# Head attention started with two groups of heads on one chunk, and lengths, statistics and last products moved in both attention layers

## The reference, cut to what matters

```python
x = x + attn_a(layernorm(x))   # 16 heads of 16; q = k = v = the normalised x, causal, softmax
x = x + ffn(layernorm(x))      # a mixture: the 2 best of 8 experts per batch, gelu
x = x + attn_b(layernorm(x))   # exp(-distance squared) of q and k, softmax over that, times v, output weights
x = x + ffn(layernorm(x))      # the same mixture again
# attn_a: w = q k^T / 4, masked to k <= q; softmax(w) v
```

## Time and profile before

| | |
|---|---|
| median of 3 runs | 1738.57 us (1738.33 to 1741.73) |
| the profiled execution, by the same clock as the runs | 1740.63 us |
| its span in the profile | 1738.9 us |
| head attention, first to last exponential | 13.5 to 532.0 us |
| first mixture | to 899 us |
| distance attention | 899 to 1367 us |
| second mixture and stores | to 1738.9 us |
| busy: PE, DVE, ACT, POOL | 97%, 59%, 55%, 18% |

### The profile page before, as it was taken

The page is one execution under the profiler, slowest core; times in us unless marked ns, Lnnn a source line. Parts: engine busy times, 40 slices in busy tenths (PEclk is TensorE's granted clock), DMA queues, the critical chain, the costliest instruction groups (busy, mean ns, idle before and its releaser), DMA issues.

```text
span 1738.9 us, 27945 instructions
## 1 busy us (share of the span) xinstructions
PE 1691.6 (97%) x10527; PEld 1156.4 (66%) x10527; DVE 1018.2 (59%) x2136; ACT 952.2 (55%) x1262; POOL 305.6 (18%) x402
## 2 busy tenths in 40 slices
PE   5999999999999999999999999999999999999998
PEld 2222222222226888888878889889899888888887
DVE  6342333344327755865566687766887886575554
ACT  4999999999996222422235444554444432243222
POOL 2022112212210000000014335434334200000000
PEclk9999999999999999999999999999999999999999
DMA  4000000100120011000000000000000200300000
GB/s 134 19 14 19 22 17 13 25 14 13 26 98 1 1 51 48 1 1 1 0 1 1 1 1 1 1 1 1 1 1 25 73 1 1 121 13 13 13 12 25
DMA packets 33697, 35.91 MB, mean 21 GB/s; under 512 B 3271, under 2 KB 30494, under 8 KB 33566
## 3 DMA queue, kind: packets, MB, share of 16 engines
q1 hardware_dynamic: 33566, 34.14, 6.6%
HBM read 22.07 MB, written 4.19 MB: 15 GB/s over the span
## 4 chain that ended last, share of the span: by engine, by line
PE 76%; ACT 11%; issue 7%; DVE 4%; POOL 0%; DMA 0%; ACTq 0%; DVEq 0%; POOLq 0%
ACT a_probs L579 10%; PE f_h L816 7%; PE f_ypsum L818 7%; PE f_ypsum L816 7%; PE a_out L386 7%; PE f_ypsum L817 7%; PE f_h L818 7%; PE f_h L817 7%; PE a_scores L700 4%; PE d_outs L816 4%; PE d_outs L817 4%; PE d_outs L818 4%; PE d_banks L816 3%; PE d_banks L818 3%; PE d_banks L817 3%
## 5 line engine op out<-in xcount | busy, mean ns | idle before, releaser
L579 ACT ACTIVATE a_probs<-a_scores 128x1024 f32<-128x1024 f32 x544 | 500.3, 1178 | 16.8 <-PE a_scores L700 16.6
L1167 ACT ACTIVATE f_gelu<-f_h,f_bcol 128x512 f32<-128x512 f32 x256 | 176.6, 690 | 467.6 <-PE f_h L818 461.2
L386 PE MATMUL a_out<-a_probs,a_values 128*32 128x512 f32 (+3 forms) x2560 | 296.0, 544 | 6.3 <-DVE a_moving L460 2.8
L1227 DVE TENSOR_SCALAR f_hh<-f_gelu,f_gates 128x512 fp32r<-128x512 f32 x256 | 124.8, 488 | 236.7 <-ACT f_gelu L1167 235.3
L1665 ACT ACTIVATE d_score<-d_dist,d_nksq 128x512 f32<-128x512 f32 x128 | 92.8, 725 | 218.9 <-DVE d_dist L1808 217.1
L1229 DVE SCALAR_TENSOR_TENSOR f_hl<-f_gelu,f_gates,f_hh 128x512 fp32r<-128x512 f32 x256 | 192.5, 752 | 9.2
L700 PE MATMUL a_scores<-a_moving,a_fixed 64*128 64x512 f16 (+3 forms) x1280 | 184.5, 355 | 9.2 <-ACT a_probs L579 4.0
L1702 POOL TENSOR_TENSOR distance_raw<-distance_raw,d_p 128x512 f32<-128x512 f32 x112 | 146.1, 1304 | 193.7 <-ACT d_p L1640 193.6
L593 POOL TENSOR_SCALAR_AFFINE_SELECT a_probs<-a_probs 128x256 f32<-128x256 f32 (+1 forms) x224 | 98.5, 455 | 431.0 <-ACT a_probs L579 428.9
L700 PEld LDWEIGHTS a_scores<-a_moving,a_fixed 64*128 64x128 f16 x1280 | 48.8, 94 | 174.6 <-ACT a_probs L579 139.3
L816 PE MATMUL f_h<-c_xhi,f_w 128*128 128x512 f32 x384 | 155.2, 404 | 0.1
(11 more groups left out here) (235 smaller groups left out, 2970.7 us busy)
## 6 DMA issues: line engine op xcount, KB each, us to landing
f_raw<-in_L_ffn_W SPq DMA_DIRECT2D x24, 512.0 KB, 7.7
a_fixed<-a_moving SPq DMA_DIRECT2D x60, 96.0 KB, 2.3
x<-in_L_attn_a_x SPq DMA_DIRECT2D x7, 512.0 KB, 8.9
out<-x SPq DMA_DIRECT2D x7, 512.0 KB, 2.9
f_raw<-in_L_ffn_W SPq DMA_DIRECT2D x12, 256.0 KB, 3.5
a_fixed<-a_moving SPq DMA_DIRECT2D x60, 32.0 KB, 2.0
f_early_raw<-in_L_ffn_W SPq DMA_DIRECT2D x4, 256.0 KB, 3.4
x<-in_L_attn_a_x SPq DMA_DIRECT2D x2, 256.0 KB, 2.8
```

Source lines behind the costliest of these rows:

```text
L386: mm = pe.matmul(spare[32 * j:32 * j + 32, i % 2, skip:skip + w], values[:, G % 2, kt + tile, j, :], probs[:, u % UR, j % 2, col:col + w], ...
L579: act.activation(probs[:, u % UR], scores[:, 2 * (u % SR):2 * (u % SR) + 2, :], ACT.Exp, scale=HD ** -0.5)\
L1167: act.activation(gel[:, n % HR, :], hps[:, n % 2, :], ACT.Gelu, bias=mix.bcol[:, q, FT * e + j:FT * e + j + 1])\
L1227: dve.tensor_scalar(hh[:, n % HR, :], gel[:, n % HR, :], gate, None, ALU.mult).then_inc(s_hh, 1)
```

## The change

1. `outputs` now begins (0,0), (1,0): the first chunk of the second group (other heads, the same tokens) is job 1 and output 1; the rest follows as before. `number` gives the place of a (`G`, `c`).
2. The `fixed` side of job 1 is copied by DVE (`place_fixed`, new semaphore `s_pfix1`) and no longer by ACT; ACT's `high_fixed(1)` stands ahead of the first unit. A chunk's steps wait for `fixed` only at its diagonal ("first"), no longer at its first full step.
3. `spare_free` is replaced by `free(bank)`, with a list of readers for each of the two banks. `TURN_AT` and the new `FIRST_TURN_AT` turn the jobs at other steps; job 2 is turned in a scores bank.
4. SP issues `copy_fixed(2)` ahead of the loads of batch 1.
5. DVE's program is written in another order: statistics, splits and places at other gaps. The statistics, norm and gathering of batch 0 stand at outputs 18, 19, 22 and 23; before they stood at 17, 19, 21, 23 and 25. A split no longer stands between a chunk's place and its `copy_out` but behind `copy_out`.
6. Distance attention: `lengths(0)` behind turn(3); several other lengths a step later, or behind a projection; the statistics of batch 0 three steps earlier (steps 73 on; before 76 on).
7. The last two weighted products (`DRAIN` = 2) are left to `finish`: one behind `up(0)`, one behind `up(1)` of the second mixture, and the denominator behind the second.

```diff
-        outputs = [(G, c) for G in range(NG) for c in range(CHUNKS)]
+        outputs = [(0, 0), (1, 0)] + [(G, c) for G in range(NG) for c in range(CHUNKS) if (G, c) not in ((0, 0), (1, 0))]
+        number = {of: i for i, of in enumerate(outputs)}
...
-        STATS_AT = {done + 1: range(TILES // 2), done + 3: range(TILES // 2, TILES)}
-        NORM_AT = done + 5
-        GATHER_AT = {done + 7: range(TILES // 2), done + 9: range(TILES // 2, TILES)}
-        MEAN_AT, CHOOSE_AT = done + 9, done + 11
+        STATS_AT = {done + 2: range(TILES // 2), done + 3: range(TILES // 2, TILES)}
+        NORM_AT, GATHER_AT, MEAN_AT, CHOOSE_AT = done + 6, done + 7, done + 9, done + 11
...
-        FIRST_TURN_AT = {5: 2, 7: 3}
-        FIRST_OUT_AT = 9
+        TURN_AT = {15: (0, (0, 1)), 16: (0, (2, 3)), 17: (1, (0,)), 18: (1, (1,)), 19: (1, (2,)), 21: (1, (3,)),
+                   26: (2, (0,)), 27: (2, (1,)), 28: (2, (2,)), 29: (2, (3,)), 30: (3, (0,)), 31: (3, (1,)), 32: (3, (2,)), 33: (3, (3,))}
+        FIRST_TURN_AT = {11: (3, (0, 1)), 12: (3, (2, 3)), 19: (4, (0,)), 20: (4, (1,)), 21: (4, (2,)), 22: (4, (3,)),
...
             load_batch(pr, sp, 0)
+            copy_fixed(BY_ENGINES)
             load_batch(pr, sp, 1)
...
             place(0)
-            statistics(1, late)
-            first_norm.rest(dve, TPC, 2 * TPC)
             normalise(1)
             halves(1)
             low_fixed(1)
+            statistics(1, late)
+            place(1)
+            first_norm.guess(dve, TPC, 2 * TPC)
+            place_fixed()
+            for i in range(3):
+                first_norm.newton(dve, i)
+            split(2)
+            copy_out(0)
+            place(2)
             statistics(2)
-            place(1)
+            finish_out(0)
+            copy_out(1)
             first_norm.rest(dve, 2 * TPC, 3 * TPC)
-            copy_out(0)
-            split(2)
...
+            finish_out(1)
             split(3)
...
+            def free(bank):
+                for s_read, count in reads[bank]:
                     pe.wait_ge(s_read, count)
+                reads[bank].clear()
...
                 if tiles[0] == 0:
-                    spare_free()
+                    if job == 2:
+                        pe.wait_ge(s_exp, 8)
+                    else:
+                        free(bank_of(job))
+                        reads[bank_of(job)].append((s_emov, job + 1))
                     pe.wait_ge(s_lo, job + 1)
...
+                if n == 1:
+                    turn(1)
                 if n == 2:
-                    turn(1)
                     turn_fixed(1)
+                if n == 5:
+                    turn(2)
...
-    LAG = 4
+    LAG, DRAIN = 4, 2
...
-              4: [("turn", 5), ("lengths", 3), ("norm", 6)],
-              5: [("values", 3), ("project", 4, 0), ("norm", 7)],
+              4: [("turn", 5), ("norm", 6)],
+              5: [("values", 3), ("lengths", 3), ("project", 4, 0), ("norm", 7)],
...
-              88: [("lengths", 15)],
+              89: [("lengths", 15)],
...
-            lengths(0)
             turn(3)
+            lengths(0)
             values(0)
-            for n in range(STEPS + LAG):
+            for n in range(STEPS + LAG - DRAIN):
...
-                if 12 <= at < 12 + TILES // 2:
+                if 9 <= at < 9 + TILES // 2:
...
-                if at == 20:
+                if at == 17:
                     next_norm.guess(dve)
...
         def finish(pe, part):
-            if part == 0:
+            weighted(pe, STEPS - DRAIN + part)
+            if part == DRAIN - 1:
                 pe.wait_ge(mix.s_bcol, 1)
                 denominator(pe, NG - 1)
```

More of the change, by code:

```diff
@@ L408, in _ @@
             distance_inputs.load(sp)
[L409 removed]
+            for job in range(BY_ENGINES + 1, CHUNKS * NG):
                 copy_fixed(job)
@@ L534, in _ @@
                         mix.part_low(dve, 0, part)
-                if i == CHUNKS + 1:
-                    for s_chunk in pr.s_x[1]:
-                        dve.wait_ge(s_chunk, 16)
-                    second_norm.whole(dve)
-                if i in STATS_AT:
-                    dve.wait_ge(s_added, CHUNKS * GROUPS)
-                    for t in STATS_AT[i]:
-                        next_norm.stats(dve, t)
-                if i == NORM_AT:
-                    next_norm.rest(dve)
-                    routing.shift(dve)
-                for t in GATHER_AT.get(i, ()):
-                    routing.gather(dve, t)
-                if i >= 1:
-                    copy_out(i)
-                    finish_out(i)
+                copy_out(i)
+                if more and c == 1:
+                    split(behind)
+                if more and c == 2:
+                    split(behind + 2)
+                if i == 2:
+                    first_norm.rest(dve, 3 * TPC, TILES)
+                finish_out(i)
                 if i == MEAN_AT:
@@ L665, in turn_fixed @@
                 mm.then_inc(s_tfix, 1)
-                routed.append((s_pfix, job + 1))
+                if job == 0:
+                    reads[1].append((s_pfix, 1))
             def turn_out(i):
-                spare_free()
+                free(i % 2)
+                reads[i % 2].append((s_added, i + 1))
                 pe.wait_ge(s_ocopy, i + 1)
```

237 lines of the change are left out of this document (132 added, 105 removed).

## The result

| | before | changed |
|---|---|---|
| median of 4 runs each, in one session | 1739.38 us (1738.33 to 1741.73) | 1726.4 us (1726.1 to 1728.75) |
| ratio of the runs | | 0.9924, interval 0.9912 to 0.9936 |
| the profiled execution, its span | 1740.63, 1738.9 us | 1726.31, 1724.3 us |
| first exponential, unit 23, table load behind the last exponential | 13.54, 48.52, 532.04 | 13.70, 38.55, 520.22 |
| first projection, last `d_dist` of the distance attention | 899.06, 1358.41 | 887.20, 1343.50 |

Faster by 0.76%, 13.0 us by the medians. Between the two profiles each landmark moved further from the one before: 10.0 up to unit 23, 1.8 from there to the last exponential, 3.05 in the distance attention, -0.3 at its end, 14.6 in all.

What follows compares the result with a forecast made beforehand. ACT was taken to bound head attention, PE distance attention. 8.9 + 1.9 + 1.7 - 0.1 = 12.4 us gained: 1728.2 from the profiled 1740.63, 1726.2 from the median 1738.57. Range 1722.8 to 1733.2.

Steps and rivals of the forecast that it cites:

- start, to unit 23: Start of head attention: 13.9 us lost before, 5.0 still lost in the new order, so 8.9 us gained.
- holes at 409 and 431: Two later ACT holes in head attention, 0.81 + 1.05, both go: 1.9 us gained, between 0 and 2.5.
- distance attention: Waits at lengths(0), (3) and (15) shrink by 0.45, 0.6 and 1.0, less 0.35: 1.7 us gained, between -1 and 2.7.
- its end: End of distance attention: DVE's chain behind the denominator is unchanged, 0.1 us lost; bounds 1.4 gained and 1.25 lost.
- u7 waits for products(1), which is as long again: 0.9: Start: the second group's unit 7 waits for PE's products(1), costing ACT 0.9 us.
- split(2) ends at 22.5 and doesn't decide: Start: DVE's split for job 2 ends at 22.5 and does not set unit 10, forecast at 26.1.
- the 1.2 that I worked out from the Trainium skill: Start: by the DVE and GpSimd port lock, about 1.2 us more lost, making the sum 7.7.
- Both causes are moved to chunks of 20 us and more: Holes at 409 and 431: the gathering and the late split move to long chunks, 1.9 us gained.
- The 0.35 for the earlier norm: Distance attention: 0.35 us taken off because batch 0's norm moves beside a chunk's results on DVE.
- the first (PE at 1.2 GHz in the start): Rival: PE stays at 1.2 GHz to u18, 5 of the 8.9 gone, gain 7, 1731.5 us; chance 0.16.
- PE is the bound: Rival: PE, not ACT, bounds head attention; gain 2 from the distance attention only, 1736.5 us; chance 0.07.
- Slower: Rival: the rest of the table is late in each head-attention group, 3.8 us worse, 1742.4 us; chance 0.05.

Runs made afterwards that it cites:

- kernel 8: The changed kernel with the second half of the gathering of batch 0 back ahead of the copy_out of output 25: 1726.17 us.
- experiment 5: The changed kernel with each chunk's first step, full or diagonal, waiting for that chunk's fixed side again: 1741.77 us, ratio to before 1.0014.
- the kernel at the end of 11: The changed kernel with DVE's guess of the norm ahead of place(1) and the first Newton step ahead of place_fixed: 1725.73 us.
- experiment 10: The changed kernel with the last job of each group turned at steps 32 to 35 as before, not 30 to 33: 1729.1 us.
- kernels 8, 9 and 10: Kernel 8, experiment 10 and, between them, the changed kernel with one list of readers for both spare banks: 1728.1 us.
- experiment 3: The changed kernel with the statistics and norm of batch 0 in the distance attention back three steps later: 1726.51 us.
- kernel 6: The kernel before, with jobs 2 to 31 awaiting their fixed side at the chunk's diagonal, not its first step: 1740.93 us, ratio 1.0006.

## Why the prediction was right, and where its steps were not

The forecast 1726.2 against 1726.4 is closer than its terms, and that much is luck. Term by term, by the two profiles:

| term | predicted | measured |
|---|---|---|
| start, to unit 23 | 8.9 | 10.0 (8.2 in the other course) |
| holes at 409 and 431 | 1.9 | 1.8 |
| distance attention | 1.7 | 3.05 |
| its end | -0.1 | -0.3 |
| sum | 12.4 | 14.6 |

- **The start, right in its mechanism.** The second group's first units fill the time in which the second chunk is made ready. This is read from the trace, where the old holes are gone; no run here undoes the order of `outputs` alone. Unit 5 at 19.6 was 19.66, partly by luck: I took 0.8 for a turn of eight transposes, though the earlier trace rows has 1.06 for one, and 1.9 for the products; measured from start to start they are 0.97 and 0.96 for the two turns (15.32 and 16.83) and 1.44 for the products (17.79). In the nine profiles with this start unit 5 lies between 18.9 and 20.0. "u7 waits for products(1), which is as long again: 0.9" failed: PE was at its higher pace by then (products at 19.77 take 1.07). "split(2) ends at 22.5 and doesn't decide" failed: it ended at 23.1, and PE waited 1.02 for it. Unit 10 came 0.8 sooner than forecast, unit 23 0.75 (38.55 for 39.3); the last wait was for `place(3)`, as forecast. In kernel 8's course unit 23 came at 40.3, so the 39.3 lies between the two.
- **What I gave no price**: that the fixed side is awaited at the diagonals. I let unit 10 follow its place at once and didn't say that this rests on the second item of the change. It carries 15 us (experiment 5). A reader of my sum could have thought that the swap alone does it.
- **DVE and POOL.** Beside masks the norm's L178 took 0.36 and not 0.17, Newton's first instruction 0.59 and not 0.16, and the normalise of four tiles 1.17 and not 0.97. These add 0.8, two thirds of the 1.2 that I worked out from the Trainium skill ("SBUF — State Buffer", on the lock of the shared port); the trace agrees with the rule, and one Newton step, not three, met a mask. (In the kernel at the end of 11, three were slowed: 0.41, 0.32 and 0.62 for 0.16.)
- **The holes.** The size was right. "Both causes are moved to chunks of 20 us and more" was wrong for the first: the eight last tiles still stand ahead of a `copy_out` (experiment 8 moves them at no gain), and what took the hole away was the turn two steps sooner (experiment 10). What took the second hole away I didn't test. It did not come back in kernels 8, 9 and 10, so it was not the place of the gathering's second half, the separate banks or the turns of the last job; the split, now ahead of `finish_out` and the mean, remains, not shown by a run. In the trace of before, DVE waits 1.89 for the mean's sums, up to 428.02, and only then makes the split at 428.10 that PE waits for the earlier trace rows.
- **The distance.** `lengths(0)` 0.48 for 0.45 and `lengths(15)` 1.06 for 1.0 were right; `lengths(3)` gave 0.30 for 0.6, as values(3) now waits 0.89 for DVE's copy. The 0.35 for the earlier norm was wrong, it costs nothing (experiment 3). Not counted at all were 6, 7, 13 and 14, together 1.2: I looked for waits that the timeline puts in brackets, and three of these four have none; one sees them only in the distance from start to start.
- **The end** was right: DVE's chain behind the denominators decides, no gain from the move. As forecast, PE's wait now stands ahead of down(0) (0.24) and up(4) (1.03). Up(4) starts 6.89 behind the denominator and not 6.61 as before, which is the 0.3.
- **The profile and the median.** I took the profiled execution to stand 2.06 above the median. Over all sessions before's medians are 1739.4 to 1740.2, so it stood 0.4 to 1.2 above, and the changed kernel's profiled execution stands at its median. By the clock of the runs the two profiled executions lie 14.3 apart (14.6 by their spans), so my terms fell short by 1.9; this and the 2.06 taken off cancel, and that is why the time came out so near. The cancelling was luck. What before's shorter runs look like stays open: its profile and that of kernel 6, which has the same start, are both of the longer kind (1740.63 and 1740.76). In the three later sessions 14 of its 35 runs lie below 1739, with a mean granted clock of 0.998 to 1.000; the others, above 1739.6, have 0.997 to 0.999. So part of the spread goes with the clock.
- **The range.** Its lower end, 1722.8, is 0.2 lower than its own bounds give (10.4 + 2.5 + 2.7 = 15.6, so 1723.0), and it takes 0 for the lower bound of the distance attention, where the term says -1.

Of the rivals, the first (PE at 1.2 GHz in the start) does occur for a few microseconds, in a third of the runs, and costs 1.7 to 1.9 us at unit 23, not 5. "PE is the bound" fell: from unit 23 to the table load it is 483.5 before and 481.7 now, which is the two holes. "Slower" named no wait that exists; the one way to the other side that does exist was experiment 5.

## What to carry to other kernels

When work is reordered so that a consumer follows its producer at once, look for every operand that takes a second way, here a copy by four DMAs 4.2 us behind the first: a wait that was free in the old order may then cost more than the reordering gives. Price small moves on a saturated engine by the distance from start to start, not by the idle time that a timeline shows. And where you shorten a wait of PE, look at the granted clock behind it, in more than one execution: behind a wait of 1.95 us in kernel 8 it fell and unit 10 came 1.5 later; behind one of 1.94 in kernel 5, and behind waits of 1.02 and 1.40, it did not fall.

## What the runs showed of the hardware that I had not expected

- The start has two courses with the same program, 1.8 us apart at unit 23 (kernel 8 and the changed kernel), by when PE's pace rises (between 17 and 19 us) and whether it falls again behind a wait (granted clock 0.50 at 24 to 26 after 1.95 idle in kernel 8; 1.00 after 1.02, after 1.40, and after 1.94 in kernel 5).
- The granted clock isn't the whole of PE's pace: in the changed kernel it is 1.00 from 16 to 18 us, where eight transposes take 1.03 (at 16.83), and 1.00 from 22 to 24 us too, where eight take 0.61 (at 23.29). Where it reads 0.50, PE is slow: products take 1.94 in kernel 8 (at 24.22), and 1.06 in the changed kernel (at 23.83), where it reads 1.00.
- Two copies of 96 KB and two of 32 KB take 2.71 us to issue on SP's queue, and 4.0 to 4.3 us pass from the end of the place to the first matmul that waits for them (kernel 5, jobs 2, 3 and 4).
